# Loading the adjacency matrix through two hardware queues, one per half of the partitions, in 1 KB packets

## The chip, the cores and the metric

The kernel runs on one core of a Trainium2 chip. The metric is device microseconds of one execution. The core has TensorE (PE), VectorE (DVE), ScalarE (ACT), GpSimd (POOL) and SyncE (SP), each with its own instruction stream, and 16 DMA engines that all queues share. SP and ACT can each issue transfers to a hardware queue of their own; POOL has a software queue.

## The reference

Two graph layers in sequence over N = 4096 nodes with D = 128 features, both with the same dense 4096 x 4096 float32 matrix `adj`:

```
h = relu(layernorm(x))
x = x + L0(h, adj, weight, bias)      # hyperbolic layer; its heart is  adj @ x_tangent
h = relu(layernorm(x))
x = x + L1(h, context, adj, ...)      # attention layer
# L0: mx = h @ weight.T; per row tanh/artanh scalings; bias added in the ball; logmap -> x_tangent
#     support = adj @ x_tangent; per row scalings, relu
# L1: in_fts = context @ W_common.T; left = in_fts @ w_left + b_left; right likewise
#     logits = leaky(left[:, None] + right[None, :], 0.2); where adj <= 0: -inf; softmax; @ h; relu
```

`adj` is 64 MB. It is read from memory once: the first layer multiplies with its values, and its signs stay on the chip as an int8 mask for the second.

## The kernel before, in words

The rows of `adj` are taken in 8 chunks c of 512 rows, the columns in 32 blocks k of 128. There is a stage ahead of the chunks and there are two phases.

*Ahead of the chunks*, x (16 transfers, `load_nodes`, L301) and the context (16 transfers) are loaded by SP, and DVE, ACT, PE and POOL work out `xt`, the tangent vectors of all nodes; the last 28 of them are finished within chunk 0 (`bias_part` on ACT, L705, and `tangent` on DVE, L970).

*Phase 1* (`load` L321, `turn` L1047, `product` L611, `signs` L750). Per block of 512 rows by 128 columns: DVE turns it (`turn_block` L875, one 32x32-block transpose of 128x512 values, into a ring of TSLOTS = 4 turned blocks), PE multiplies `xt[:, k]` with it into a bank of PSUM (L619), and ACT writes the signs of two turned blocks into the mask (L758). A turned slot is free again when PE and ACT have read it. DVE's instruction order is fixed: beside the transposes of chunk c stand the steps that finish chunk c - 1 (`post_steps`, L979), each behind a block of a given number: relu behind 7, sums behind 12 and 13, `shrink` (L1001) behind 17, `residual` (L1016) behind 21 and 22, `variance` (L1034) behind 25, `affine` (L1040) behind 29. Two of them need POOL: `norms` (L514, between L996 and L1001) and `inverse_std` (L518, between L1034 and L1040). Between these POOL does the preparation of the second layer in pieces (`beside`, L503): eight pieces `left_or_right` (L452 and L457), then the sums and a store of `neg_left` to memory in 4-byte elements (L465), the largest value, and exponentials. ACT finishes a chunk with `normed` (L743), four instructions behind the last sign of the next chunk.

Loading: SP alone issues `adj`. A tile of the load ring is 16 rows by 128 columns for each partition (512-byte packets), 1 MB, four blocks k; the ring has XSLOTS = 4 tiles. A tile is four transfers of 256 KB, one for each group b of 32 partitions, and its place is asked for when DVE has turned all four blocks of the tile that was there (L328). Between tiles SP also issues the store (`store_x1`, L307) and the load (`load_x`, L313) of 512 rows of x.

*Phase 2* (`attend` L626, `edges` L779, `split` L1098) is the attention product over the mask; it loads only rows of x and of `neg_left`, and PE, DVE and ACT share it.

A node's number is made of (s, b, l, q): chunk s, group b of 32 partitions, l of 4, q within the group; this order is used for rows, columns, x, context and the output alike.

Of the kernel before, what the change touches and what calls it, by code (L numbers as in the profile page):

```python
# [44 lines left out]
Q = 32  # L45
NQ = P // Q
L = 4
CH = L * P
XSLOTS = 4
# [4 lines left out]
BESIDE = 8  # L54

# [21 lines left out]
def bass_two_graph_layers(nc, x, adj, weight, bias, context, w_common, w_left, b_left, w_right, b_right, out):  # L77
# [3 lines left out]
    NC = N // CH  # L81
    TH = NC * HALVES
# [3 lines left out]
    with ExitStack() as ctx:  # L86
# [10 lines left out]
        phase_1_bytes = XT_BYTES + XSLOTS * CH * L * 4 + TSLOTS * CH * 4  # L97
# [32 lines left out]
        loaded = view(room, o, [XSLOTS, L * NQ, L * Q], F32)  # L130
        o += XSLOTS * CH * L * 4
# [8 lines left out]
        assert nl_at == 4 * half_slot and (NC - XSLOTS) % XSLOTS == 0  # L140
# [97 lines left out]
        def nodes(t):  # L238
            return t.rearrange("(s b l q) d -> s b q l d", b=NQ, l=L, q=Q)

        x_n, out_n = nodes(x), nodes(out)
        x_l, cx_l = (t.rearrange("(s b l q) d -> l b q s d", b=NQ, l=L, q=Q) for t in (x, context))
        adj_n = adj.rearrange("(s r p) (g b j) -> s g b p r j", r=CH // Q, p=Q, b=NQ, j=L * Q)
# [56 lines left out]
        def _(sp):  # L300
            def load_nodes(t, src, into):  # L301
# [3 lines left out]
            load_nodes(x_in, x_l, x_in_sem)  # L305
# [15 lines left out]
            def load(c, _):  # L321


                rows = pick(adj_n, c)
                for g in range(NC):
                    if not (isinstance(c, int) and c == 0 and g < XSLOTS):

                        sp.wait_ge(block_turned, c * NK + L * (g - XSLOTS + 1))  # L328
                    for b in range(NQ):
                        sp.dma_start(loaded[b * Q:(b + 1) * Q, g % XSLOTS], rows[g, b]).then_inc(  # L330
                            adj_in[g % XSLOTS], 16)
                    if isinstance(c, int) and c == 0 and g == XSLOTS - 1:
                        load_nodes(cx, cx_l, cx_in)
# [14 lines left out]
            sp.wait_ge(block_turned, NC * NK - (XSLOTS - 1) * L)  # L348
# [220 lines left out]
        def _(pe):  # L569
# [85 lines left out]
        def _(act):  # L655
            act.dma_start(W_in, weight).then_inc(weights_in, 16)
            act.dma_start(b_colv, bias.rearrange("(d a) -> d a", a=1)).then_inc(weights_in, 16)
            act.dma_start(bias_b, bias.rearrange("(a d) -> a d", a=1).broadcast_to([P, D])).then_inc(weights_in, 16)

# [45 lines left out]
            def bias_part(k):  # L705

                if k >= XT_AHEAD:
                    act.wait_ge(xt_ready, k - XT_AHEAD + 1)
                nc.scalar.activation(fb[:, k % XT_AHEAD, :], hb, ACT.Copy, scale=sv[:, 14, k:k + 1]).then_inc(
                    fb_ready, 1)  # L710
# [39 lines left out]
            def signs(c, parity):  # L750
# [3 lines left out]
                mc = mask[:, c] if number else mask[:, bass.ds(c, 1)].rearrange("p o k i -> p (o k) i")  # L754
                for half in range(TH):
# [78 lines left out]
        def _(dve):  # L834
# [40 lines left out]
            def turn_block(c, k):  # L875
                g, l = k // L, k % L
                if l == 0:
                    dve.wait_ge(adj_in[g % XSLOTS], c * (16 * NQ * NC // XSLOTS) + 16 * NQ * (g // XSLOTS + 1))
# [91 lines left out]
            def tangent(k):  # L970

                dve.wait_ge(fb_ready, k + 1)
                v.scalar_tensor_tensor(out=xt[:, k, :], in0=mx[:, k, 0:D], scalar=T1[:, k:k + 1],  # L973
                                       in1=fb[:, k % XT_AHEAD, :], op0=ALU.mult, op1=ALU.add).then_inc(xt_ready, 1)
# [72 lines left out]
            def turn(c, parity):  # L1047
                number = isinstance(c, int)
                steps = {} if number and c == 0 else post_steps(c - 1)
                for k in range(NK):  # L1050
                    if not (number and c == 0 and k < TSLOTS):
                        turn_block(c, k)
                    if number and c == 0:
                        tangent(k)
# [144 lines left out]
```

## Time and profile before

| | us |
|---|---|
| median of 3 runs | 674.5 (673.03 to 675.14) |
| the profiled execution's own time | 676.54 |
| its span | 674.7 |

Mean granted clock of TensorE 0.941 of full speed. Busy shares of the span: PE 76%, DVE 81%, ACT 63%, POOL 34%. The page cuts the span into 40 slices of 16.9 us. DMA traffic is nearly all in slices 1 to 23, which are the stage ahead and phase 1; phase 2 follows, from about 386 us to the end. In windows of less than the span the same line has 40 slices of that window. "Idle before, releaser" tells what ended an engine's idle time; idle time of an engine that is not the bottleneck costs nothing.

### The profile page before, as it was taken

What the parts mean: (1) busy time and instruction counts of PE and PEld (TensorE: products, weight loads), DVE (VectorE), ACT (ScalarE), POOL (GpSimd) and SP (SyncE); (2) the same over time, 40 slices, a digit from 0 to 9 for tenths busy, and PEclk for the clock granted to TensorE, in tenths of its full rate; (3) what the DMA queues carried; (4) which work ended last, traced back from release to release, by engine and by line L of the source; (5) the groups of instructions that cost most, each with busy time, mean ns of one, the idle gap of its engine ahead of it and who ended that gap; (6) DMA issues with size and microseconds to landing.
All of it is one profiled execution on the core that took longest, in us unless ns stands there. A gap on an engine that the chain in (4) does not pass through costs nothing. (4 is left out here: it accounts for less than half of the span.)

```text
span 674.7 us, 9733 instructions
## 1 busy us (share of the span) xinstructions
PE 512.0 (76%) x2695; PEld 312.2 (46%) x2695; DVE 545.3 (81%) x1057; ACT 422.5 (63%) x553; POOL 226.9 (34%) x217
## 2 busy tenths in 40 slices
PE   1705986597589478687786855669998989899995
PEld 1602432242233223222232244458877878787875
DVE  4897957989697366574665799999999999999995
ACT  2946954273356245445354487849898888879881
POOL 5810067949948168000000075720101020202010
PEclk9966999799799699999999968888999999999998
DMA  9995999999999999999999701010101001011010
GB/s 180 214 223 111 213 214 213 222 213 213 181 217 152 169 216 225 213 213 223 214 219 215 141 17 32 1 32 17 32 17 33 18 30 47 16 31 31 0 31 16
DMA packets 164235, 84.51 MB, mean 125 GB/s; under 512 B 7248, under 2 KB 163152, under 8 KB 164208
## 3 DMA queue, kind: packets, MB, share of 16 engines
q1 hardware_dynamic: 163520, 83.91, 69.4%
q0 software_dynamic: 256, 0.15, 0.1%
q8 instruction: 11, 0.18, 0.1%
q10 hardware_dynamic: 432, 0.13, 0.1%
q14 instruction: 16, 0.13, 0.1%
HBM read 79.96 MB, written 4.21 MB: 125 GB/s over the span
## 5 line engine op out<-in xcount | busy, mean ns | idle before, releaser
L619 PE MATMUL ps<-room 128*128 128x512 f32 x512 | 254.0, 633 | 94.9 <-DVE room L884 72.5
L884 DVE STREAM_TRANSPOSE room<-room 128x512 f32<-128x512 f32 x256 | 169.6, 692 | 91.2 <-DMA room<-in_adj_dram 78.1
L758 ACT ACTIVATE mask<-room 128x1024 f32 (+1 forms) x128 | 135.0, 1055 | 160.0 <-DVE room L884 158.0
L619 PEld LDWEIGHTS ps<-room 128*128 128x128 f32 x512 | 93.8, 198 | 249.6 <-DVE room L884 168.6
L645 PE MATMUL ps<-room 128*128 128x258 f16 x1152 | 139.3, 282 | 29.6 <-DVE room L1126 29.6
L645 PEld LDWEIGHTS ps<-room 128*128 128x128 bf16 x1152 | 114.0, 100 | 53.6 <-DVE room L1126 35.2
L645 PE MATMUL ps<-room,mask 128*128 128x258 f16 x896 | 102.5, 275 | 9.4 <-DVE h_room L1140 6.3
L645 PEld LDWEIGHTS ps<-room,mask 128*128 128x128 bf16 x896 | 87.0, 98 | 23.6 <-DVE h_room L1140 8.0
L797 ACT ACTIVATE room<-mask 128x2048 bf16 (+1 forms) x36 | 68.5, 1902 | 13.9 <-PE ps L645 13.9
L554 POOL TENSOR_TENSOR h_room<-h_room 128x512 f32<-128x512 f32 x7 | 9.9, 1408 | 146.4 <-DVE post L1151 146.4
L797 ACT ACTIVATE mask<-mask 128x2048 bf16 (+1 forms) x28 | 53.3, 1903 | 5.0 <-PE ps L645 5.0
L452 POOL TENSOR_TENSOR mask<-mask 128x2048 f32<-128x2048 f32 x8 | 36.1, 4512 | 50.7 <-DVE room L973 50.5
L1116 DVE TENSOR_TENSOR room<-room 128x2048 bf16<-128x2048 bf16 x36 | 48.4, 1344 | 1.3 <-ACT room L797 0.4
L457 POOL TENSOR_TENSOR mask<-mask 128x1024 f32<-128x1024 f32 (+3 forms) x64 | 46.5, 726 | 5.0
L514 POOL TENSOR_TENSOR post<-post,powers 128x8 f32<-128x8 f32 x8 | 13.4, 1670 | 98.0 <-DVE post L996 98.0
L1116 DVE TENSOR_TENSOR mask<-mask 128x2048 bf16<-128x2048 bf16 x28 | 34.7, 1238 | 1.1
L827 ACT ACTIVATE h_room<-ps,factors 128x258 f32<-128x258 f32 x32 | 14.0, 471 | 33.0 <-PE ps L645 21.3
L1070 DVE TENSOR_SCALAR room<-room,r_col 128x512 bf16<-128x512 f32 x42 | 27.1, 686 | 0.0
L1125 DVE TENSOR_SCALAR room<-room 128x2048 bf16<-128x2048 bf16 x36 | 25.5, 708 | 0.2
L1126 DVE TENSOR_SCALAR room<-room 128x2048 bf16<-128x2048 bf16 x36 | 25.4, 704 | 0.0
L806 ACT ACTIVATE room<-room,r_col 128x512 bf16<-128x512 f32 x38 | 25.1, 709 | 0.0
L518 POOL TENSOR_TENSOR post<-post,powers 128x4 f32<-128x4 f32 x8 | 8.3, 1036 | 43.8 <-DVE post L1034 43.6
(164 smaller groups left out, 552.9 us busy)
## 6 DMA issues: line engine op xcount, KB each, us to landing
room<-in_adj_dram SPq DMA_DIRECT2D x256, 256.0 KB, 6.8
mask<-in_L_gnn_context_dram SPq DMA_DIRECT2D x16, 256.0 KB, 10.6
mask<-in_x_dram SPq DMA_DIRECT2D x16, 128.0 KB, 5.7
xk<-in_x_dram SPq DMA_DIRECT2D x32, 64.0 KB, 4.4
out_dram<-xk SPq DMA_DIRECT2D x32, 64.0 KB, 4.2
h_room<-out_dram SPq DMA_DIRECT2D x32, 64.0 KB, 2.5
out_dram<-h_room SPq DMA_DIRECT2D x28, 64.0 KB, 1.8
room<-neg_left SPq DMA_DIRECT2D x4, 256.0 KB, 3.6
```

Of the source, the lines that this page charges most:

```text
L452: side(nc.gpsimd.tensor_tensor(products, cx[:, ks, :], v_rows[:, w, :].unsqueeze(1).broadcast_to([P, BESIDE, C]), ALU.mult))
L457: side(nc.gpsimd.tensor_tensor(dst, products[:, :, 0:n], products[:, :, n:2 * n], ALU.add))
L619: pe.matmul(acc[parity], xt[:, k, :], turned[:, k % TSLOTS, :], start=(k == 0), stop=(k == NK - 1)).then_inc(block_multiplied, 1)
L645: mm = pe.matmul(ps[:, 2 * t + w, 0:GW], part[slot(c, g)][:, kk, t * P:(t + 1) * P], G[w][:, k, :], start=(k == 0), stop=(k == NK - 1))
L758: nc.scalar.activation(mc[:, half * HB:(half + 1) * HB, :], turned[:, slots:slots + HB, :], ACT.Sign).then_inc(half_signed, 1)
L797: nc.scalar.activation(neg[slot(c, g)], mc[:, g * L:(g + 1) * L, :], ACT.Relu, scale=4.0).then_inc(edges_ready, 1)
L806: ins = nc.scalar.activation(pos[slot(c, g)][:, kk, :], nl[parity], ACT.Sign, scale=-1.0, bias=r_col[:, k:k + 1])
L884: v.transpose(turned[:, k % TSLOTS, :].rearrange("p (l b i) -> p b l i", l=L, b=NQ), loaded[:, g % XSLOTS, :, l * Q:(l + 1) * Q].rearrange ...
L1070: ins = v.tensor_scalar(pos[slot(c, g)][:, kk, :], nl[parity], r_col[:, k:k + 1], -1.0, ALU.is_le, ALU.add)
L1116: v.tensor_tensor(pos_g, pos_g, neg_g, ALU.add).then_inc(coded, 1)
L1125: v.tensor_scalar(neg_g, pos_g, 3.0, None, ALU.is_equal)
L1126: v.tensor_scalar(pos_g, pos_g, 4.0, None, ALU.is_ge).then_inc(parts_ready, 1)
```

## The change

SP issues the transfers of partitions 0 to 63 (`LOW`), ACT those of partitions 64 to 127 (`HIGH`), for x and for `adj`; the context stays with SP. A tile of `adj` becomes 16 rows by 256 columns for each partition (1 KB packets), 2 MB, eight blocks, and the ring has two tiles (the same room). Transfers of `adj` are 512 KB; there are 128 of them, where there were 256. ACT issues a tile's high half behind the last sign of the tile that it replaces (in the last tile of a chunk also behind `normed`), and its loop over the chunks is written out. SP's store and load of x rows move from tiles 1 and 3 of 8 to tiles 0 and 1 of 4.

Node numbers are now made of (b, l, s, q). So a partition's 16 rows of a tile are 256 rows (4 MB of memory) apart, where they were 32 rows (512 KB), and the four groups b read columns 1024 apart. The columns of block k are those of xt and mask place `node(k)`; the mask is written with a stride.

```
-XSLOTS = 4
+XSLOTS = 2
+XB = 8
+LOW, HIGH = range(NQ // 2), range(NQ // 2, NQ)
+    NT = NK // XB
...
-        loaded = view(room, o, [XSLOTS, L * NQ, L * Q], F32)
+        loaded = view(room, o, [XSLOTS, L * NQ, XB * Q], F32)
...
-        adj_n = adj.rearrange("(s r p) (g b j) -> s g b p r j", r=CH // Q, p=Q, b=NQ, j=L * Q)
+        x_l, cx_l = (t.rearrange("(b l s q) d -> l b q s d", b=NQ, l=L, q=Q) for t in (x, context))
+        adj_n = adj.rearrange("(r s p) (b g j) -> s g b p r j", s=NC, p=Q, b=NQ, j=XB * Q)
+        def node(n):
+            return n % XB * L + n // XB
...
-                for g in range(NC):
+                for g in range(NT):
                     if not (isinstance(c, int) and c == 0 and g < XSLOTS):
-                        sp.wait_ge(block_turned, c * NK + L * (g - XSLOTS + 1))
-                    for b in range(NQ):
-                        sp.dma_start(loaded[b * Q:(b + 1) * Q, g % XSLOTS], rows[g, b]).then_inc(
-                            adj_in[g % XSLOTS], 16)
+                        sp.wait_ge(block_turned, c * NK + XB * (g - XSLOTS + 1))
+                    for b in LOW:
+                        sp.dma_start(loaded[b * Q:(b + 1) * Q, g % XSLOTS], rows[g, b]).then_inc(adj_in[g % XSLOTS], 16)
...
-                    if g == 1 and not (isinstance(c, int) and c < 2):
+                    if g == 0 and not (isinstance(c, int) and c < 2):
                         store_x1(c - 2)
-                    if g == 3 and not (isinstance(c, int) and c < 1):
+                    if g == 1 and not (isinstance(c, int) and c < 1):
                         load_x(c - 1)
...
-                    pe.matmul(acc[parity], xt[:, k, :], turned[:, k % TSLOTS, :],
+                    pe.matmul(acc[parity], xt[:, node(k), :], turned[:, k % TSLOTS, :],
...
+            def load_high(rows, g):
+                for b in HIGH:
+                    act.dma_start(loaded[b * Q:(b + 1) * Q, g % XSLOTS], rows[g, b]).then_inc(adj_in[g % XSLOTS], 16)
+            for l in range(L):
+                for b in HIGH:
+                    act.dma_start(by_l(x_in, l)[b * Q:(b + 1) * Q], x_l[l, b]).then_inc(x_in_sem[l], 16)
+            for g in range(XSLOTS):
+                load_high(adj_n[0], g)
...
                 for half in range(TH):
                     act.wait_ge(block_turned, c * NK + HB * (half + 1))
                     slots = half % HALVES * HB
-                    nc.scalar.activation(mc[:, half * HB:(half + 1) * HB, :], turned[:, slots:slots + HB, :],
+                    first = node(half * HB)
+                    nc.scalar.activation(mc[:, first:first + L + 1:L, :], turned[:, slots:slots + HB, :],
                                          ACT.Sign).then_inc(half_signed, 1)
...
                     if half in steps:
                         steps[half]()
+                    if (half + 1) % (XB // HB) == 0:
+                        tile = half // (XB // HB) + XSLOTS
+                        if tile < NT:
+                            load_high(rows, tile)
+                        elif further is not None:
+                            load_high(further, tile - NT)
-            chunked(act, signs)
+            for c in range(NC):
+                signs(c, c % 2)
...
             def turn_block(c, k):
-                g, l = k // L, k % L
+                g, l = k // XB, k % XB
```

## Rows read from the trace of the kernel before

**Rows 1.** The page: DMA busy tenths and GB/s in 40 slices.
```profile
DMA  9995999999999999999999701010101001011010
GB/s 180 214 223 111 213 214 213 222 213 213 181 217 152 169 216 225 213 213 223 214 219 215 141 17 32 1 32 17 32 17 33 18 30 47 16 31 31 0 31 16
```

**Rows 2.** Waits of all engines: waiter, awaited, us in total, times, longest.
```profile
DVE room L884 <- DMA room<-in_adj_dram: 78.1, 37, 10.7
```

**Rows 3.** Groups by line: shapes, count, busy us, mean ns, idle before, releasers.
```profile
L884 DVE STREAM_TRANSPOSE room<-room 128x512 f32<-128x512 f32 x256 | 169.6, 692 | 91.2 <-DMA room<-in_adj_dram 78.1 <-PE ps L619 8.6 <-ACT mask L758 2.4
L758 ACT ACTIVATE mask<-room 128x1024 f32 (+1 forms) x128 | 135.0, 1055 | 160.0 <-DVE room L884 158.0
```

**Rows 4.** Windows of 10 us: busy per engine, clock, DMA share, GB/s.
```profile
40.00:50.00 10.00, 0.00 (x0) 0.00 (x0) 8.48 (x37) 5.58 (x10) 0.00 (x0) 0.50 1.13 224
70.00:80.00 10.00, 10.00 (x25) 4.38 (x24) 10.00 (x24) 9.64 (x18) 0.00 (x0) 1.00 1.22 213
320.00:330.00 10.00, 6.80 (x15) 2.44 (x15) 6.78 (x13) 3.59 (x6) 1.64 (x1) 1.00 1.23 213
```

**Rows 5.** DMA view of 241 to 245 us, 0.1 us a slice.
```profile
GB/s 220 215 195 210 210 200 205 210 200 200 225 241 266 230 220 220 205 215 215 210 179 205 205 195 215 215 210 205 195 200 205 220 205 210 205 230 251 271 225 195
```

**Rows 6.** DMA view of 1.5 to 9.5 us, 0.2 us a slice.
```profile
GB/s 0 77 115 164 325 341 287 226 157 141 90 100 102 74 143 120 187 223 228 300 272 295 272 270 203 187 144 168 223 185 132 178 159 146 173 244 228 205 236 213
```

**Rows 7.** Timeline of 300 to 345 us: start, us, engine, line, what, idle before.
```profile
309.94 2.49 DVE L884 STREAM_TRANSPOSE room<-room 128x512 f32<-128x512 f32 x4 [2.28 <-DMA room<-in_adj_dram]
310.71 3.70 PE L619 MATMUL ps<-room 128*128 128x512 f32 x8 [0.63 <-DVE room L884]
...
318.31 0.19 PEld L619 LDWEIGHTS ps<-room 128*128 128x128 f32 x1 [0.24 <-issue]
...
318.74 0.19 PEld L619 LDWEIGHTS ps<-room 128*128 128x128 f32 x1 [0.24 <-issue]
```

**Rows 8.** Source view of the adj transfers: issue durations ns, then issue to landing.
```profile
L330 SPq DMA_DIRECT2D room<-in_adj_dram x256: 311/980/8402, 9.9 to 375.5; - x128
...
DMA to landing us min/median/max: 3.2/6.8/15.9
```

**Rows 9.** Timeline of 0 to 24 us: a DMA issued by ACT.
```profile
1.68 0.46 ACTq L658 DMA_DIRECT2D mask<-in_L_gnn_bias_dram  x1
```

**Rows 10.** Groups by line of ACT, 230 to 385 us.
```profile
L743 ACT ACTIVATE h_room<-xk,post 128x128 f32 x12 | 4.9, 478 | 0.0
```

**Rows 11.** Timeline of POOL, 75 to 240 us.
```profile
104.98 1.65 POOL L514 TENSOR_TENSOR post<-post,powers 128x8 f32<-128x8 f32 x1 [8.02 <-DVE post L996]
...
117.62 4.50 POOL L452 TENSOR_TENSOR mask<-mask 128x2048 f32<-128x2048 f32 x1
...
128.62 1.02 POOL L518 TENSOR_TENSOR post<-post,powers 128x4 f32<-128x4 f32 x1
...
149.54 1.65 POOL L514 TENSOR_TENSOR post<-post,powers 128x8 f32<-128x8 f32 x1 [9.00 <-DVE post L996]
...
194.01 1.65 POOL L514 TENSOR_TENSOR post<-post,powers 128x8 f32<-128x8 f32 x1 [8.88 <-DVE post L996]
```

**Rows 12.** Timeline of DVE, 134 to 300 us.
```profile
129.67 4.46 DVE L1040 SCALAR_TENSOR_TENSOR post<-mv,post 128x4 f32<-128x4 f32 x1 [0.70 <-POOL post L518]
...
211.92 0.12 DVE L1040 SCALAR_TENSOR_TENSOR post<-mv,post 128x4 f32<-128x4 f32 x1
...
227.50 2.49 DVE L884 STREAM_TRANSPOSE room<-room 128x512 f32<-128x512 f32 x4 [10.68 <-DMA room<-in_adj_dram]
```

**Rows 13.** Timeline of POOL, 230 to 340 us.
```profile
240.88 1.69 POOL L514 TENSOR_TENSOR post<-post,powers 128x8 f32<-128x8 f32 x1 [10.06 <-DVE post L996]
...
281.80 1.64 POOL L514 TENSOR_TENSOR post<-post,powers 128x8 f32<-128x8 f32 x1 [13.26 <-DVE post L996]
```

**Rows 14.** DMA view of 205 to 232 us: issues, KB, median us to landing.
```profile
neg_left<-mask POOLq DMA_DIRECT2D x1, 16.0 KB, 18.3
```

**Rows 15.** The chain of waits: start, us, piece.
```profile
384.40 1.23 DVE room L884 x2
```

More of the change, by code:

```diff
@@ L96, in bass_two_graph_layers @@
         XT_BYTES = NK * D * 4
-        phase_1_bytes = XT_BYTES + XSLOTS * CH * L * 4 + TSLOTS * CH * 4
+        phase_1_bytes = XT_BYTES + XSLOTS * CH * XB * 4 + TSLOTS * CH * 4
         phase_2_bytes = 2 * NK * GW * 2 + 3 * 2 * L * CH * 2
@@ L129, in bass_two_graph_layers @@
         o += NK * D * 4
[L130 to L131 removed]
+        loaded = view(room, o, [XSLOTS, L * NQ, XB * Q], F32)
+        o += XSLOTS * CH * XB * 4
         turned = view(room, o, [TSLOTS, CH], F32)
@@ L139, in bass_two_graph_layers @@
         nl_at = XT_BYTES
-        assert nl_at == 4 * half_slot and (NC - XSLOTS) % XSLOTS == 0
+        assert nl_at == 4 * half_slot and NT % XSLOTS == 0
         nl_even = view(room, nl_at, [CH], F32)
@@ L238, in nodes @@
         def nodes(t):
-            return t.rearrange("(s b l q) d -> s b q l d", b=NQ, l=L, q=Q)
+            return t.rearrange("(b l s q) d -> s b q l d", b=NQ, l=L, q=Q)
         x_n, out_n = nodes(x), nodes(out)
-        x_l, cx_l = (t.rearrange("(s b l q) d -> l b q s d", b=NQ, l=L, q=Q) for t in (x, context))
-        adj_n = adj.rearrange("(s r p) (g b j) -> s g b p r j", r=CH // Q, p=Q, b=NQ, j=L * Q)
+        x_l, cx_l = (t.rearrange("(b l s q) d -> l b q s d", b=NQ, l=L, q=Q) for t in (x, context))
+        adj_n = adj.rearrange("(r s p) (b g j) -> s g b p r j", s=NC, p=Q, b=NQ, j=XB * Q)
+        def node(n):
+            return n % XB * L + n // XB
         def pick(view_, c):
@@ L300, in _, with load_nodes @@
         def _(sp):
-            def load_nodes(t, src, into):
+            def load_nodes(t, src, into, blocks):
                 for l in range(L):
-                    for b in range(NQ):
+                    for b in blocks:
                         sp.dma_start(by_l(t, l)[b * Q:(b + 1) * Q], src[l, b]).then_inc(into[l], 16)
-            load_nodes(x_in, x_l, x_in_sem)
+            load_nodes(x_in, x_l, x_in_sem, LOW)
             def store_x1(p):
@@ L324, in load @@
                 rows = pick(adj_n, c)
-                for g in range(NC):
+                for g in range(NT):
                     if not (isinstance(c, int) and c == 0 and g < XSLOTS):
-                        sp.wait_ge(block_turned, c * NK + L * (g - XSLOTS + 1))
-                    for b in range(NQ):
-                        sp.dma_start(loaded[b * Q:(b + 1) * Q, g % XSLOTS], rows[g, b]).then_inc(
-                            adj_in[g % XSLOTS], 16)
+                        sp.wait_ge(block_turned, c * NK + XB * (g - XSLOTS + 1))
+                    for b in LOW:
+                        sp.dma_start(loaded[b * Q:(b + 1) * Q, g % XSLOTS], rows[g, b]).then_inc(adj_in[g % XSLOTS], 16)
                     if isinstance(c, int) and c == 0 and g == XSLOTS - 1:
-                        load_nodes(cx, cx_l, cx_in)
-                    if g == 1 and not (isinstance(c, int) and c < 2):
+                        load_nodes(cx, cx_l, cx_in, range(NQ))
+                    if g == 0 and not (isinstance(c, int) and c < 2):
                         store_x1(c - 2)
-                    if g == 3 and not (isinstance(c, int) and c < 1):
+                    if g == 1 and not (isinstance(c, int) and c < 1):
                         load_x(c - 1)
@@ L346, in _ @@
             sp.wait_ge(nl_stored, 16)
-            sp.wait_ge(block_turned, NC * NK - (XSLOTS - 1) * L)
+            sp.wait_ge(block_turned, NC * NK - (XSLOTS - 1) * XB)
             neg_left_row(0, 0)
@@ L708, in bias_part @@
                     act.wait_ge(xt_ready, k - XT_AHEAD + 1)
-                nc.scalar.activation(fb[:, k % XT_AHEAD, :], hb, ACT.Copy, scale=sv[:, 14, k:k + 1]).then_inc(
+                at = node(k)
+                nc.scalar.activation(fb[:, k % XT_AHEAD, :], hb, ACT.Copy, scale=sv[:, 14, at:at + 1]).then_inc(
                     fb_ready, 1)
@@ L754, in signs @@
                 mc = mask[:, c] if number else mask[:, bass.ds(c, 1)].rearrange("p o k i -> p (o k) i")
+                rows = pick(adj_n, c)
+                further = None if number and c == NC - 1 else adj_n[c + 1] if number else pick(adj_n, c + 1)
                 for half in range(TH):
@@ L969, in _, with tangent @@
             dve.wait_ge(tangent_scales, 1)
-            def tangent(k):
-                dve.wait_ge(fb_ready, k + 1)
+            def tangent(n, k):
+                dve.wait_ge(fb_ready, n + 1)
                 v.scalar_tensor_tensor(out=xt[:, k, :], in0=mx[:, k, 0:D], scalar=T1[:, k:k + 1],
-                                       in1=fb[:, k % XT_AHEAD, :], op0=ALU.mult, op1=ALU.add).then_inc(xt_ready, 1)
+                                       in1=fb[:, n % XT_AHEAD, :], op0=ALU.mult, op1=ALU.add).then_inc(xt_ready, 1)
             POST = 6
@@ L1053, in turn @@
                     if number and c == 0:
-                        tangent(k)
+                        tangent(k, node(k))
                     if k in steps:
```

2 lines of the change are left out of this document (1 added, 1 removed).

## The prediction, made before the changed kernel was run

> **What bounds the kernel now.** I read the page's slices first. The DMA digits are at 9 or near it from slice 1 to slice 23 and almost nothing after; in the full slices the core moves 213 to 216 GB/s, and it moves no more in any slice than 225 [rows 1]. So the change can act on the first 386 us only, and there the question is who waits for the loads. By the waits, DVE stands 78.1 us for `adj`, in 37 waits, the longest 10.7 us [rows 2]; nothing else holds its transposes for long (8.6 and 2.4 us), and ACT in turn waits 158.0 us for DVE [rows 3]. 78.1 us is the ceiling of the gain, unless something else speeds up as well.
>
> Is 213 GB/s a limit of the packet, of memory, or of where the data lands? Three readings. The context is loaded in 1 KB packets to 32 partitions at a time and goes at 224 GB/s, `adj` in 512-byte packets at 213 [rows 4]: twice the packet gives 5%. Seen in slices of 0.1 us, the `adj` stream has two humps in 4 us, 241-266-230 and 251-271-225, 2.5 us apart [rows 5]. A transfer of 256 KB takes 1.23 us at 213 GB/s, so a hump stands at every second change of transfer, not at each: that fits changes between the lower and the upper 64 partitions, where for some 0.3 us both are being written, and not those within a half. And early, where the loads of x share the DMA engines with 128-partition loads of ACT and POOL, slices reach 287 to 341 and 270 to 300 GB/s with packets mostly of 512 bytes [rows 6]. I take it that one half of the partitions takes in some 213 to 224 GB/s, and that both together take more.
>
> The Trainium skill speaks on both sides here. "SBUF — State Buffer", section "Door 1", gives 8 of 16 ports and about 218 GB/s to partitions 0 to 63; the trace agrees with 213 to 224. The same page, section "Can I just issue two DMAs to hit both halves?", says no: two at a time gained 6%, and "DMA: Bandwidth & Descriptors", section "Rules for kernel authors", says of two transfers to disjoint halves not to bother. The humps speak against that for this stream, and it is the first rival below.
>
> **The change part by part.**
>
> *The rate R with both halves open.* Bounds from the nearest rows: 213 (nothing gained) and 341 (the highest slice). The humps' 266 and 271 are the same loads, but averaged over a moment that is partly one-sided, and with the smaller packet. I take R = 290, with 250 and 340 as the forecast's own ends.
>
> *The ring of two tiles.* A tile (2.1 MB) is asked for when the eight blocks in its place are turned, and has to be there when the other tile has been turned. If L is the time from that release to the landing and T the time DVE needs for a landed tile, two tiles take L + T, unless DVE, PE or the DMA engines need more. T: four transposes take 2.49 us [rows 7], eight 5.0; in 320 to 330 us DVE is busy 6.78 us [rows 4] with 8.1 blocks (5.0 us of transposes), so 1.7 us of other steps per tile: T = 6.7. L: the shortest landing of 256 KB is 3.2 us [rows 8], less 1.2 of data at 213: 2.0 fixed. Data: 2.1 MB at 290, 7.2 us. ACT issues the high half behind its sign (1.055 us, [rows 3]) and one issue of 0.46 [rows 9]; meanwhile the low half is alone at about 213, which costs 1.5 x (1 - 213/290) = 0.4. In the last tile of a chunk `normed`, 4 x 0.48 us [rows 10], stands ahead too: a quarter of about 1.4, 0.35. L = 10.0. So a tile takes (10.0 + 6.7)/2 = 8.35 us, 1.044 per block. The other limits are lower: PE's records start 0.43 us apart, two to a block, 0.86 per block [rows 7]; the data alone is 7.2 us per tile. With R = 340, L = 9.0 and a block takes 0.98; with 250, L = 11.2 and a block 1.12.
>
> *ACT's issues.* Two per tile, 0.92 us at the 0.46 of its own row. Behind them stand the next signs, which DVE needs four blocks later. Per tile in the late chunks ACT then has 4.2 of signs, about 1 of other steps and 0.9 of issues in 8.35 us: hidden. At most two tiles' high halves, four transfers, are ever outstanding, and SP had 6.8 / 1.23 = 5.5 in flight before an issue was held (its median issue of 980 ns is that hold, its minimum 311) [rows 8]; so I cost no hold. If that cover is gone, an issue costs ACT what it cost SP, about 1 us, 8.4 at worst.
>
> *Stage ahead.* x arrives over both halves; its first group has to wait for ACT's three small loads (0.46 each). I cost -0.5 to +1, zero. ACT's first compute instruction waits for DVE's statistics of x, which need x landed, and so stands well behind its issues.
>
> *Chunk 0.* ACT is saturated (9.64 of 10 us busy, [rows 4]) with signs and `bias_part`. Four times 0.92 us of issues go on top: +3.7. The two-tile ring adds about 1 at its third tile, mostly beside it. Behind chunk 0 DVE used to wait some 8 us for loads before block 13 of chunk 1; there I get it back, and `norms` starts about 105, as before (104.98, [rows 11]).
>
> *Chunks 1 to 3: POOL's.* This is where the expected gain stays away. From `norms` at 104.98 POOL runs two pieces of 10.9 (one starts with the 4.50 at 117.62) and ends `inverse_std` at 129.64: 24.7 us [rows 11]. Then `affine` on DVE stands 4.46 us [rows 12], as long as POOL's next L452. These 29.1 us cover blocks 14 to 29, which need 14 to 18 us of loads' or DVE's time: faster loads change nothing. The other 16 blocks take 15.4 us (to 149.54), already PE's pace, 0.86 to 0.96 a block, from tiles that were loaded during the stand. With the two-tile ring only blocks up to 7 of the next chunk are there; block 31 is turned 1.2 us behind the stand's end, its place lands 10.0 + 1.1 later, and block 8 wants it at +9.4: +2 us for each such half chunk. The period was 44.5 (149.54 to 194.01); I take 46.5, twice: 198.
>
> *The end of that stretch.* Blocks 14 to 29 of chunk 3 took 17.9 us (194.01 to 211.92), bound by DVE and its stands: 18, so 216. Then 29.0 us to the next `norms` at 240.88 [rows 13]: here the store of `neg_left` in 4-byte elements is in flight for 18.3 us [rows 14], and DVE waits 10.68 us for `adj` [rows 12]. Undisturbed this stretch costs 15.4 + 2. Two queues with twice the packet put more `adj` bytes between two turns of the store; nothing in the trace prices it. Between 17.4 and 29 I take 22: 238.
>
> *Chunks 4 to 7.* From `norms` at 240.88 to the last transpose's end at 385.63 [rows 15] are 144.8 us for 115 blocks (1.26 each; a chunk 40.9, by 281.80 - 240.88). At 1.044: 120.1, so 358.
>
> *The rest.* Phase 2 has no part in the change: the strided mask write, `node(k)` and the written-out ACT loop add no instruction per block; 0, at most ±1.
>
> **The sum.** Phase 1 ends at 358 in place of 385.6: -27.6. The profiled execution took 676.54 for a span of 674.7, 2.0 above the median of the runs shown; 676.5 - 27.6 = 648.9, and on the median's scale 674.5 - 27.6 = 647. By terms: chunk 0 and the start 0, chunks 1 and 2 +4, the `neg_left` stretch -7, chunks 4 to 7 -24.7. Best ends together (R = 340, no ring loss, 17.4 in the `neg_left` stretch) give 632; worst (R = 250, 29 there, +3 at chunk 0) 669.
>
> **Rivals.**
>
> *The halves don't add.* If each engine works its two queues off in turn and every packet waits for its port, R stays at the context's 224 [rows 4]. Then the data of a tile is 9.4 us, L = 12.2, and a tile takes 9.45: 1.19 per block, 136.5 us for the 115; the early half chunks lose 4.5 instead of 2, the `neg_left` stretch 27: 385, that is 674, up to 681 if the engines idle in part of L. For it: the pages above, and that the engines are shared. Against it: [rows 5, 6].
>
> *Memory at a stride of 4 MB (the slower side).* A partition's 16 rows of a tile are now 4 MB apart, 512 KB before. If rows so far apart meet in the same part of memory, R falls for every `adj` transfer. From about R = 224 down this decides: 63 MB are to come, so each 10% off costs 28 us, and 200 GB/s gives about 708. Against it: neighbouring partitions, which the 16 engines read side by side, stay 16 KB apart; no row shows a stride above 512 KB. The Trainium skill, "DMA: Bandwidth & Descriptors", section "Latency and other measured facts", has half the rate for a pitch of 4 MiB against 512 KiB, but between the partitions of a transfer; no row here shows it, and by its half R would be near 110 and the time above 900.
>
> *ACT is held by its issues.* If two transfers of 512 descriptors cost ACT more than about 2.5 us per tile, it paces DVE and comes late with the high half; 28 tiles with 1 us too much are 28 us, and the time lands between 650 and 690. For it: SP's 980 ns and 8.4 us. Against it: only four transfers outstanding.
>
> *More than forecast.* R near 340 and the `neg_left` stall gone: below 634.
>
> **Chances.** Forecast 0.56 (own range 634 to 669, all of it faster); better 0.06; halves don't add 0.17 (faster 0.03, no change 0.05, slower 0.09); stride 0.09, slower; ACT held 0.12 (0.06, 0.01, 0.05). A measurement of this kernel tells about 0.3% (2 us) from no change. Faster 0.71, no change 0.06, slower 0.23. The range runs from 632, with 0.05 below, to 682, which holds most of the first rival and leaves out the stride and half of ACT's bad end, some 0.13.
>
> **What would show it.** Right: two hardware queues with about equal bytes and slices of 280 to 300 GB/s in chunks 4 to 7, with gaps between tiles; `norms` 46 us apart in chunks 1 to 3 and some 33 apart in 4 to 7; DVE's waits for `adj` of 1.5 to 3 us, once per eight blocks. Wrong: slices that stay at 213 to 224 (first rival) or fall below (second); ACT's DMA issues of 1 us and more (third); `norms` less than 44 us apart in chunks 1 to 3, which would mean that POOL did not bound them; or a phase 2 of another length than 289 us.

## The result: 880 us, slower by 31%, and the profile after

The changed kernel takes 880.24 us (median of 4 runs, 875.07 to 881.91), the kernel before in the same session 673.76 (671.54 to 675.14). The ratio is 1.306, interval 1.299 to 1.312. The forecast of 647 was wrong in its sign; the time lies far outside the range of 632 to 682. Ratios here and below compare runs near each kernel's fastest; a single run that took clearly longer than its others is given with its time.

The page of the profiled execution (875.07 us, span 873.3): DMA busy tenths and GB/s in 40 slices, now of 21.8 us each, and the DMA queues with packets, MB and share of the 16 engines.

```profile
DMA  7914786577777887778767877720000101001000
GB/s 200 246 48 53 145 145 136 123 124 133 129 132 155 120 59 165 107 136 159 154 117 143 168 110 161 134 73 1 25 25 18 33 26 37 12 24 36 24 23 13
...
q1 hardware_dynamic: 59968, 49.30, 29.0%
q10 hardware_dynamic: 36400, 34.74, 21.9%
```

The same bytes go over two queues, as meant. But where [rows 1] has 213 to 216 GB/s, there are now 107 to 168 in the full slices (59 in slice 15, where the store of `neg_left` is in flight), and the DMA digit stands mostly at 7 or 8, not 9. Phase 1's loads run to slice 27 of 21.8 us, where they ran to slice 23 of 16.9 us.

The view of waits, all engines, then SP's queue (waiter, awaited, us, times, longest):

```profile
DVE room L912 <- DMA room<-in_adj_dram: 260.9, 30, 19.2
...
SPq L326 <- DMA out_dram<-xk: 66.9, 6, 15.3
```

DVE's wait for `adj` has grown from 78.1 us in 37 waits [rows 2] to 260.9 in 30, by 183 us. The span has grown by 198.6. SP's wait at L326 is for a store of x rows that shares the slow stream; behind it stands SP's half of the next tile. Of DVE's 260.9 us, 217.9 are put down to SP's halves and 43.0 to ACT's. Experiment 1 will show that the loss comes without this wait too. The rest is shown by POOL's `norms` (L520, L514 before), one per chunk:

```profile
147.43 1.65 POOL L520 TENSOR_TENSOR post<-post,powers 128x8 f32<-128x8 f32 x1 [17.38 <-DVE post L1024]
213.90 1.65 POOL L520 TENSOR_TENSOR post<-post,powers 128x8 f32<-128x8 f32 x1 [28.39 <-DVE post L1024]
283.16 1.65 POOL L520 TENSOR_TENSOR post<-post,powers 128x8 f32<-128x8 f32 x1 [23.78 <-DVE post L1024]
357.57 1.69 POOL L520 TENSOR_TENSOR post<-post,powers 128x8 f32<-128x8 f32 x1 [11.64 <-DVE post L1024]
424.11 1.64 POOL L520 TENSOR_TENSOR post<-post,powers 128x8 f32<-128x8 f32 x1 [21.18 <-DVE post L1024]
488.25 1.64 POOL L520 TENSOR_TENSOR post<-post,powers 128x8 f32<-128x8 f32 x1 [37.28 <-DVE post L1024]
...
549.04 1.64 POOL L520 TENSOR_TENSOR post<-post,powers 128x8 f32<-128x8 f32 x1 [35.11 <-DVE post L1024]
```

A chunk takes 61 to 74 us where it took 41 to 47 [rows 11, 13], in POOL's chunks as in the later ones. The last transposes of phase 1 start at 582.31 and take 1.48 us, so it ends at 583.8 in place of 385.6: 198.2 of the 198.6 us. Phase 2 takes 289.5 us, as before. So the loss lies in phase 1, in the loads: that is the second rival's picture (memory at a stride of 4 MB), which had a chance of 0.09. What follows had to show whether it was the stride, or one of the other things that the change did to the loads.

### The profile page after: what moved, and what is told of

Read it like the earlier page. It is cut to its first block, busy times and chain, and to the rows that moved or that the text cites. A ratio compares the mean times of both kernels' runs of the same rounds, so it can differ in the third digit from the quotient of the medians.

```text
span 873.3 us, 9067 instructions
## 1 busy us (share of the span) xinstructions
PE 550.2 (63%) x2695; PEld 335.0 (38%) x2695; DVE 532.8 (61%) x1057; ACT 422.8 (48%) x553; POOL 227.0 (26%) x217
## 4 chain that ended last, share of the span: by engine, by line
DMA 41%; DVE 31%; PE 12%; issue 7%; SPq 4%; ACTq 2%; ACT 2%; POOL 1%; DVEq 1%; POOLq 0%
DMA room<-in_adj_dram 38%; PE ps L625 9%; DVE room L1098 4%; DVE room L1144 4%; DVE mask L1098 3%; DVE room L912 3%; DVE room L1154 3%; DVE mask L1144 3%; DMA out_dram<-xk 3%; PE ps L651 2%; SPq L318 2%; DVE mask L1154 2%; ACTq L669 1%; SPq L337 1%; DVE h_room L1168 1%
## 5 line engine op out<-in xcount | busy, mean ns | idle before, releaser
L625 PE MATMUL ps<-room 128*128 128x512 f32 x512 | 289.2, 723 | 247.6 <-DVE room L912 209.6
L912 DVE STREAM_TRANSPOSE room<-room 128x512 f32<-128x512 f32 x256 | 171.6, 696 | 298.0 <-DMA room<-in_adj_dram 260.9
L779 ACT ACTIVATE mask<-room 128x1024 int8<-128x1024 f32 x128 | 135.0, 1055 | 354.2 <-DVE room L912 353.4
L625 PEld LDWEIGHTS ps<-room 128*128 128x128 f32 x512 | 113.7, 231 | 414.7 <-DVE room L912 290.4
L651 PE MATMUL ps<-room 128*128 128x258 f16 x1152 | 141.9, 285 | 28.4 <-DVE room L1154 28.4
L520 POOL TENSOR_TENSOR post<-post,powers 128x8 f32<-128x8 f32 x8 | 13.4, 1669 | 174.8 <-DVE post L1024 174.8
## 6 DMA issues: line engine op xcount, KB each, us to landing
room<-in_adj_dram ACTq DMA_DIRECT2D x64, 512.0 KB, 17.4
```

The source lines that it names most:

```text
L625: pe.matmul(acc[parity], xt[:, node(k), :], turned[:, k % TSLOTS, :], start=(k == 0), stop=(k == NK - 1)).then_inc(block_multiplied, 1)
L651: mm = pe.matmul(ps[:, 2 * t + w, 0:GW], part[slot(c, g)][:, kk, t * P:(t + 1) * P], G[w][:, k, :], start=(k == 0), stop=(k == NK - 1))
L779: nc.scalar.activation(mc[:, first:first + L + 1:L, :], turned[:, slots:slots + HB, :], ACT.Sign).then_inc(half_signed, 1)
L912: v.transpose(turned[:, k % TSLOTS, :].rearrange("p (l b i) -> p b l i", l=L, b=NQ), loaded[:, g % XSLOTS, :, l * Q:(l + 1) * Q].rearrange ...
```

## The experiments

Four things changed in the loads: the distance of a partition's rows, the packet with the groups' columns apart, the tile and ring, the two queues. Theory A: the distance alone. Theory B: two queues or the small ring. Theory C: the columns.

**1. The distance alone, on the kernel before.**

```
-adj_n = adj.rearrange("(s r p) (g b j) -> s g b p r j", r=CH // Q, ...)
+adj_n = adj.rearrange("(r s p) (g b j) -> s g b p r j", s=NC, ...)
```

> The kernel before (one queue, 512-byte packets, four tiles), with one thing changed: the 16 rows of adj that a partition takes in a tile are 256 rows (4 MB) apart instead of 32 (512 KB). The product is then with wrongly ordered rows. Theory A (memory serves rows 4 MB apart slowly, and that alone made the changed kernel slow): adj falls from 213 GB/s to what the changed kernel shows, 120 to 160, and the time goes to 800 to 900 us. Theory B (two rings on the same 16 DMA engines get in each other's way, or the two-tile ring exposes each landing): nothing changes, 674 us within 5. Theory C (the four groups reading columns 4 KB apart): 674 us too.

Measured: 888.35 us (884.83 to 891.42), ratio 1.317, interval 1.310 to 1.324. One queue, small packets and the old ring, and yet the whole loss. Its waits, and two windows of 20 us (busy per engine, clock, DMA share, GB/s):

```profile
DVE room L884 <- DMA room<-in_adj_dram: 323.3, 57, 15.1
...
320.00:340.00 20.00, 11.85 (x22) 5.27 (x23) 7.20 (x13) 6.87 (x10) 0.65 (x2) 0.67 0.60 128
...
400.00:420.00 20.00, 11.47 (x23) 4.52 (x23) 6.03 (x10) 6.11 (x9) 0.00 (x0) 0.76 0.65 128
```

128 GB/s in place of 213, with the engines' share at 0.60 to 0.65 instead of 1.22 [rows 4]. The packets themselves are not recorded as longer. SP's queue in the kernel before, then in this one (packets, MB, share of 16 engines' span):

```profile
q1 hardware_dynamic: 163520, 83.91, 69.4%
```

```profile
q1 hardware_dynamic: 163520, 83.91, 48.1%
```

That is 45.8 ns a packet (0.694 x 16 x 674.7 us by 163520) against 41.9. The time lost stands between the recorded packets, so a DMA share that falls need not mean that the engines had too little to do.

**2. The changed kernel without the distance.**

```
-adj_n = adj.rearrange("(r s p) (b g j) -> s g b p r j", s=NC, ...)
+adj_n = adj.rearrange("(s r p) (b g j) -> s g b p r j", s=NC, ...)
```

> The changed kernel (two queues, 1 KB packets, two tiles of 2 MB), with one thing undone: a partition's 16 rows are 512 KB apart again; the groups' columns stay 1024 apart. Rows and columns are then in different orders, so the product is of wrongly ordered rows. Theory A: the two halves add, slices of 280 to 300 GB/s in chunks 4 to 7, and the sum of the prediction holds, plus some 9 us for ACT's held issues at the start: 640 to 670 us. Theory B: 850 to 880 us as the changed kernel. Theory C: 850 to 880 as well.

Measured: 662.28 us (659.10 to 667.56), ratio 0.983, interval 0.975 to 0.991. With one access pattern undone, 218 us are gone; theories B and C fall. The DMA view of 340 to 360 us, 0.5 us a slice:

```profile
GB/s 238 240 344 352 346 336 219 330 365 264 240 350 346 340 225 234 338 352 352 340 352 312 213 230 221 242 262 336 352 350 270 225 242 354 346 344 354 180 29 106
```

Here the forecast's mechanism can be read off: plateaus of mostly 336 to 354, with both queues carrying equal bytes (0.10 MB each in 341.2 to 341.8 us), and valleys of 213 to 242. Split by queue, the valleys are of two kinds. In some one queue carries nearly all: ACT's 0.08 MB against 0.02 from 340.0 to 340.4, SP's alone 0.11 MB from 343.0 to 343.5 and from 351.0 to 351.5, there in packets of some 512 bytes, those of x rows. In others both carry the same (0.04 MB each from 340.4 to 340.8, 0.06 from 345.0 to 345.5) and the rate is 218 to 240 all the same; that isn't explained. The mean of the window is 287 GB/s; I had taken 290.

**3. The change's first part alone: two queues.**

```
-                    for b in range(NQ):
+                    for b in LOW:
                         sp.dma_start(loaded[...], rows[g, b])
...
+                    if half % HALVES == HALVES - 1:      # ACT, behind the sign of a tile's last blocks
+                        ...load_high(...)
```

> The kernel before with SP issuing adj for partitions 0 to 63 and ACT for 64 to 127, behind its sign of a tile's last two blocks; 512-byte packets, four tiles of 1 MB, rows and columns in the old order, x by SP alone. Theory A: the halves add; R about 265 (the humps), chunks 4 to 7 about 33 us each instead of 41, time 640 to 660. Theory B: slower than 700. Theory C: 640 to 660.

Measured: 648.77 us (647.38 to 653.92), ratio 0.966, interval 0.959 to 0.972. The order of nodes, the packets and the ring are the old ones. The later `norms` are 30.5 to 31.6 us apart, where 33 was expected. It is also 13.5 us faster than experiment 2, so the longer packet in a ring of two tiles brought nothing that shows.

**4. 1 MB on the kernel before.**

```
-adj_n = adj.rearrange("(s r p) (g b j) -> s g b p r j", ...)
+adj_n = adj.rearrange("(t r h p) (g b j) -> t h g b p r j", h=2, ...)   # chunk c: t = c // 2, h = c % 2
```

> The kernel before with a partition's 16 rows 64 rows (1 MB) apart instead of 512 KB, SP's loop over the chunks written out for it; the product is of wrongly ordered rows. Theory A with a cost that grows with the stride: between 680 and 780 us; theory A with a cost that begins above 1 MB: 674 within 5. Theories B and C: 674 within 5.

Measured: 675.03 us (10 runs, 672.58 to 677.41), ratio 1.001, interval 0.999 to 1.004. One queue moves some 213 GB/s here and so would hide a loss that begins above that.

**5. The same distance, not a power of two.** Two accounts of "4 MB" were left: it is far, or it is an exact power of two.

```
-adj.rearrange("(r s p) ...")                       # r: 256 rows
+adj[0:16 * 255].rearrange("(r x) ...", x=255)[...]  # r: 255 rows, 4 MB less 16 KB
```

> The changed kernel with one thing changed: a partition's 16 rows are 255 rows apart, 4 MB less 16 KB, instead of 256 (each chunk reads 32 rows of 16 such stripes; the product is of wrongly ordered rows). The bytes, the packets, the queues, the tiles and the distance are as in the changed kernel. Theory A1 (rows an exact multiple of a large power of two apart meet in the same part of memory): as with 512 KB, 655 to 670 us, and packets of 1 KB take some 46 to 60 ns in the middle and under 100 at the ninth decile. Theory A2 (it is the distance: anything some MB apart is slow, whatever the exact number): 850 to 890 us.

Measured: 792.74 us (790.81 to 796.30), ratio 1.179, interval 1.173 to 1.185. Neither account: 88 us better than 256 rows, 130 worse than 32.

**6. Half the distance, on the changed kernel.**

```
-adj_n = adj.rearrange("(r s p) (b g j) -> s g b p r j", s=NC, ...)
+adj_n = adj.rearrange("(t r h p) (b g j) -> t h g b p r j", h=4, ...)   # chunk c: t = c // 4, h = c % 4
```

> The changed kernel with a partition's 16 rows 128 rows (2 MB) apart instead of 256 (wrongly ordered rows). Theory A1, if each doubling of the stride halves the number of places that a tile's rows fall on: between 690 and 800 us. If the cost begins only at 4 MB: 655 to 670. A2 says between 700 and 850.

Measured: 760.76 us (five runs at 754.54 to 764.51; the profiled one took 904.57 at a granted clock of 0.564, and its profile isn't read), ratio 1.130, interval 1.125 to 1.135.

**7. A whole kernel with 1 KB packets and 1 MB.** Nodes numbered (t, b, l, h, q), chunk c = 2t + h: the 256 columns of a packet stay adjacent, and the 16 rows are 64 apart.

```
-"(b l s q) d -> s b q l d"      adj "(r s p) (b g j) -> s g b p r j"
+"(t b l h q) d -> t h b q l d"  adj "(t r h p) (g b j) -> t h g b p r j"
```

> A whole kernel with the change's two queues, 1 KB packets and two tiles of 2 MB, but nodes numbered so that a partition's 16 rows are 64 rows (1 MB) apart and the four groups' columns of a tile lie side by side; x and the context are loaded in twice as many transfers for it. If 1 MB costs nothing at the rate of two queues either: 655 to 668 us, as with 512 KB. If 1 MB costs some of the rate above 213 GB/s, which one queue could not show: 670 to 720.

Measured: 669.92 us (10 runs, 667.23 to 676.47), ratio 0.996, interval 0.992 to 1.000. It is 8 us above experiment 2; that the stride costs these isn't separated from the 32 transfers more at the start.

From here a rule could be formed. A matrix row is 16 KB. The 32 rows that the partitions of a group take cover the lowest five bits of the row number. 32, 64, 128 and 256 rows between a partition's own rows let bits 5 to 7 take 8, 4, 2 and 1 values within a chunk; 255 rows, where row = 256r + (p - r) from the chunk's first row on, two, with about three quarters of the rows in one of them. The times were 662, 670, 761, 880 and 793. The bits are a description that fits these times, not a known address map. A rule with bit 8 added (16, 8, 4, 2 and 4 values) ranks the five no differently, and the part of bit 5 rests on the 8 us just named.

**8. The rule tested: 3.5 MB.**

```
-stripes of 255 rows
+stripes of 224 rows (7 x 32: all eight values of bits 5 to 7)
```

> The changed kernel with a partition's 16 rows 224 rows (3.5 MB) apart (chunk c reads the first 32 rows of 16 such stripes from row 32 c on, some rows twice over the kernel; wrongly ordered). What the runs suggest so far: a matrix row is 16 KB, and memory is spread by bits of the row number above the lowest five; 32, 64, 128, 256 rows apart leave 8, 4, 2, 1 different values of bits 5 to 7 in one chunk's rows, 255 leaves 2, and the times were 662, 670, 761, 880, 793. 224 = 7 x 32 leaves all 8. By that theory 655 to 670 us. By the theory that distance costs (more than 2 MB apart is slow): 790 to 900.

Measured: 659.69 us (659.37 to 668.25), ratio 0.981, interval 0.975 to 0.987. Nearly as far as 4 MB, and as fast as 512 KB. Distance is not it. (With bit 8 added, 224 rows have all values too.) The page's slices:

```profile
GB/s 195 285 168 0 140 193 265 204 122 272 221 121 269 171 90 241 238 284 286 275 272 275 96 1 31 1 33 17 33 17 33 40 20 35 16 31 31 0 31 16
```

**9. The start.** In experiments 2 and 3 ACT began late. The timeline of ACT in experiment 3:

```profile
2.17 13.41 ACTq L663 DMA_DIRECT2D room<-in_adj_dram  x8
15.62 1.28 ACT L684 ACT_TABLE_LOAD   x1 [15.62 <-issue]
18.07 1.65 ACT L684 ACTIVATE mask<-mask 128x128 f32<-128x128 f32 x4 [1.18 <-DVE mask L856]
```

Eight transfers took ACT 13.41 us, 1.68 each: a hold like SP's [rows 8], now in front of ACT's first work. The edit: SP issues the first four tiles whole.

> The version with two queues, 512-byte packets and four tiles, with the first four tiles issued whole by SP, so that ACT issues no adj ahead of its first compute instruction. If ACT's held issues at the start (its first compute instruction came at 15.6 and 18.1 us there instead of 12.8) cost what they delay, 2 to 3 us come back: 645 to 647. If they were hidden, or if the first tiles come later through one queue, nothing: 648.8 within 2.

Measured: 638.92 us (three runs at 635.59 to 639.13, one at 658.30), ratio 0.947, interval 0.941 to 0.953. It gave 10 us, not 2 to 3. The first `norms` of experiment 3 and of this version:

```profile
107.08 1.65 POOL L515 TENSOR_TENSOR post<-post,powers 128x8 f32<-128x8 f32 x1 [3.28 <-DVE post L1011]
```

```profile
98.49 1.65 POOL L515 TENSOR_TENSOR post<-post,powers 128x8 f32<-128x8 f32 x1 [3.09 <-DVE post L1008]
```

8.6 of the 10 are there: ACT's first compute instruction comes 5 us earlier (at 13.10), and chunk 0 starts sooner. The edit took away two things at once, though. In experiment 3 x itself landed later, since ACT's `adj` transfers moved beside it. DVE's first instruction on x, of experiment 3 and of this version:

```profile
10.46 1.65 DVE L864 BATCH_NORM_STATS2 mask<-mask 128x6 f32<-128x128 f32 x8 [10.46 <-DMA mask<-in_x_dram]
```

```profile
8.20 1.64 DVE L861 BATCH_NORM_STATS2 mask<-mask 128x6 f32<-128x128 f32 x8 [8.20 <-DMA mask<-in_x_dram]
```

So some 2.3 of the 5 us are x's landing and some 2.7 ACT's hold. This is the version to take; it beats both kernels.

**10. The store in 4-byte elements.**

```
-pool.dma_start(nl_dram.rearrange("k p -> p k"), neg_l, ...)
+pool.dma_start(nl_dram, ident[0:NK, :])
```

> The version with two queues, 512-byte packets and the first tiles by SP, with the store of neg_left (16 KB in 4096 elements of 4 bytes) replaced by one of the same size in 32 rows of 512 bytes from another tile, at the same place of POOL's order; the second layer then works with wrong numbers. DVE waited 9.9 us for adj in one piece in that stretch. If the small elements alone hold the DMA engines: the stretch between the third and the fourth norms falls from 48 to 33 to 38 us and the time from 639 to 625 to 630. If the stretch is long for another reason (POOL's reduction of the maximum): 639 within 3.

Measured: 631.44 us (630.68 to 634.54), ratio 0.937, interval 0.934 to 0.940. The third and the fourth `norms`, of experiment 9 and of this one:

```profile
188.48 1.65 POOL L515 TENSOR_TENSOR post<-post,powers 128x8 f32<-128x8 f32 x1 [9.18 <-DVE post L1008]
...
229.29 0.38 POOL L475 PARTITION_ALL_REDUCE mask<-mask  x1 [12.55 <-issue]
237.03 1.68 POOL L515 TENSOR_TENSOR post<-post,powers 128x8 f32<-128x8 f32 x1 [7.37 <-issue]
```

```profile
187.90 1.65 POOL L515 TENSOR_TENSOR post<-post,powers 128x8 f32<-128x8 f32 x1 [9.07 <-DVE post L1008]
...
222.10 0.38 POOL L475 PARTITION_ALL_REDUCE mask<-mask  x1 [6.11 <-issue]
229.89 1.68 POOL L515 TENSOR_TENSOR post<-post,powers 128x8 f32<-128x8 f32 x1 [7.41 <-issue]
```

48.6 us become 42.0, not 33 to 38: the store costs 6.6 us. Behind it stands the other thing I had named. The fourth `norms` follows an idle time of 7.4 us that ends in "issue", so POOL itself came late from its reduction, not DVE. The store's 6.6 us come by the same way: POOL's idle time ahead of the reduction is 12.55 us with the small elements and 6.11 without.

The DMA engines suffer as well, and here ACT was held a second time. The stretch in experiment 9, ACT and then DVE:

```profile
210.95 5.81 ACTq L663 DMA_DIRECT2D room<-in_adj_dram  x1
...
216.79 5.10 ACTq L663 DMA_DIRECT2D room<-in_adj_dram  x1
221.93 1.06 ACT L763 ACTIVATE mask<-room 128x1024 int8<-128x1024 f32 x1 [9.21 <-issue]
```

```profile
224.07 2.49 DVE L896 STREAM_TRANSPOSE room<-room 128x512 f32<-128x512 f32 x4 [8.72 <-ACT mask L763]
```

Two issues of ACT took 5.81 and 5.10 us, its next sign stood 9.21 us behind them, and DVE stood 8.72 us for the sign. With the store in rows no issue there takes more than 0.51 us, and from 200 to 232 us the core moves 260 GB/s in place of 174. In experiment 9 this hold stays under POOL's reduction: DVE's sums are there at 231.2 us, POOL comes at 237.0.

**11. Halves or queues?**

```
-LOW, HIGH = range(NQ // 2), range(NQ // 2, NQ)
+LOW, HIGH = (0, 2), (1, 3)
```

> The same version with the groups dealt out otherwise: SP issues the partitions 0 to 31 and 64 to 95, ACT 32 to 63 and 96 to 127, so each queue has work in both halves and the two queues begin in the same half. If the gain comes from both halves being written at a time: the queues run side by side within one half, and the time goes back towards 674, to 655 to 675. If two queues gain by themselves, whatever their partitions: 639 within 4.

Measured: 661.11 us (658.36 to 665.61), ratio 0.981, interval 0.976 to 0.985. Against experiment 9 this gives back 22 us, though two queues issue the same transfers. Windows of 20 us, of experiment 9 (10 us each) and of this one:

```profile
310.00:320.00 10.00, 9.81 (x22) 3.85 (x22) 9.14 (x24) 7.72 (x11) 1.01 (x1) 1.00 1.20 276
320.00:330.00 10.00, 10.00 (x27) 4.48 (x26) 7.08 (x12) 6.57 (x9) 0.00 (x0) 1.00 1.20 281
```

```profile
300.00:320.00 20.00, 17.42 (x42) 6.76 (x40) 12.35 (x20) 11.99 (x16) 1.64 (x1) 1.00 1.21 253
```

253 GB/s is more than 213. That the queues drift apart and both halves are then open in part is my reading; no run shows it.

**12. One queue, halves in turn.**

```
-for b in range(NQ):
+for b in (0, 2, 1, 3):
```

> The kernel before with SP alone issuing a tile's four transfers in the order of groups 0, 2, 1, 3 instead of 0, 1, 2, 3, so that every transfer changes the half. If both halves can only be open at a change of transfer, for 0.3 us each as in the humps: there are twice as many changes, R goes from 213 to 220 to 235, time 655 to 668. If one queue keeps both halves open as well as two do (the engines get out of step): 640 to 650. If order means nothing: 674 within 3.

Measured: three runs at 664.92 to 666.82 and one at 648.70, against 674.49 before, all four at the same granted clock (0.944 to 0.945). The three are inside what I expected of twice as many changes, the fourth inside what I expected if one queue keeps both halves open as well as two do. So order means something, but which of the two accounts holds isn't settled. The profile is of a run of 664.92 us. Its DMA view of 241 to 245 us, 0.1 us a slice, to be laid beside [rows 5]:

```profile
GB/s 230 246 225 215 220 215 246 236 236 236 236 236 251 220 241 225 230 230 225 220 230 241 210 241 230 241 230 205 225 241 230 230 225 246 225 251 230 220 225 215
```

The valleys between the humps, down to 179, are gone; all slices are at 205 to 251, with a mean of 230. So order alone in one queue is worth some 8 to 10 us in three runs and 26 in the fourth, against 25 for the two queues on halves in experiment 3 and 35 in experiment 9.

## Why the prediction was wrong, step by step

**The step that failed is R.** "The rate R with both halves open" was bounded below at 213, "nothing gained", by rows of loads whose rows lay 512 KB apart at most. The change moved them to 4 MB, and I kept this out of the term and made it a rival at 0.09. R was 107 to 168. From 75 us, where the first tile behind the two of the start is issued, to 576 us, where the last has landed, the core moves 134 GB/s on the mean; the 30 tiles take 501 us, 16.7 each and 2.09 per block, where the forecast had 7.2 us of data in 8.35 us a tile and 1.044 per block. The measured rate accounts for the result: phase 1 ends at 583.8 and not at 358.

The first rival has a slip beside it: at R = 224 its L adds up to 11.8, not 12.2, since the low half's lead costs 0.1 there and not 0.4. That moves its 674 by some -4 us and decides nothing.

The reason that I gave against the rival was wrong as a reason. "Neighbouring partitions stay 16 KB apart" is true, and it covers only five bits of the row number; experiments 5, 6 and 8 show that bits above them matter. And I let "no row shows a stride above 512 KB" count against the rival, when it was only silence. A rate that only untested addresses would have should have widened the range downward, as I did for other costs without a row.

The Trainium skill had spoken: "DMA: Bandwidth & Descriptors", section "Latency and other measured facts", gives 207 GB/s at a row pitch of 512 KiB, 164 at 2 MiB and 103 at 4 MiB, measured between the partitions of copies. I set it aside because here the stride is within a partition. In this kernel too 4 MB gives 128 GB/s where 512 KB gives 213 (experiment 1), a factor of 0.60 against the 0.50 of the Trainium skill; by that half I had worked out over 900 us, and 880 came. The Trainium skill's remedy in the same place, a pitch off by 4 KiB, can't be tried within a partition, since a row of `adj` is 16 KB; the nearest to it, 16 KB less, brought 88 of 218 us back, and 512 KB less all of it. As to the rule of the Trainium skill, "DMA: Bandwidth & Descriptors", section "Rules for kernel authors", that two transfers to disjoint halves are not worth it, the measurement decides the other way for this stream: plateaus of 336 to 354 GB/s with both queues at work against 213 to 242, and 25 us of 674 in experiment 3, 35 in experiment 9.

**The other steps** can be checked on experiment 2, which differs from the changed kernel in the distance alone. POOL's `norms` there, one a chunk:

```profile
112.21 1.65 POOL L520 TENSOR_TENSOR post<-post,powers 128x8 f32<-128x8 f32 x1 [6.26 <-DVE post L1024]
...
158.36 1.65 POOL L520 TENSOR_TENSOR post<-post,powers 128x8 f32<-128x8 f32 x1 [10.52 <-DVE post L1024]
...
205.21 1.65 POOL L520 TENSOR_TENSOR post<-post,powers 128x8 f32<-128x8 f32 x1 [11.22 <-DVE post L1024]
...
258.66 1.69 POOL L520 TENSOR_TENSOR post<-post,powers 128x8 f32<-128x8 f32 x1 [9.00 <-DVE post L1024]
...
292.74 1.64 POOL L520 TENSOR_TENSOR post<-post,powers 128x8 f32<-128x8 f32 x1 [6.86 <-DVE post L1024]
...
325.17 1.64 POOL L520 TENSOR_TENSOR post<-post,powers 128x8 f32<-128x8 f32 x1 [17.91 <-DVE post L1024]
...
357.06 1.64 POOL L520 TENSOR_TENSOR post<-post,powers 128x8 f32<-128x8 f32 x1 [17.53 <-DVE post L1024]
```

- *Chunks 1 to 3, POOL's:* 46.2 and 46.9 us, predicted 46.5. Faster loads give nothing there. The two-tile ring costs its 2 us or near it: with four tiles (experiment 9) the same two periods are 45.2 and 44.8.
- *Chunks 4 to 7:* 34.1, 32.4 and 31.9, predicted 33.4. Right.
- *Start and chunk 0:* first `norms` at 112.21, predicted 105. Two terms at zero failed. ACT's issues ahead of its first work were costed at nothing, but its eight transfers of x took 7.27 us and the four of `adj` behind them 8.04, so its first work starts at 17.53. And x over both halves was costed at -0.5 to +1, but DVE's first instruction on it starts at 10.62 and not at 7.88, with `adj` loads beside it.
- *The stretch with the `neg_left` store:* 53.5 us, predicted 40. I expected two queues with larger packets to push past the store. They don't: DVE waits 19.09 us there in one piece. The floor of 17.4 us that I gave the second half of the stretch was wrong too: with the small elements gone the stretch is still 42.0 us (experiment 10), and POOL's reduction, which had no term in the sum, ends it.

```profile
243.54 2.49 DVE L912 STREAM_TRANSPOSE room<-room 128x512 f32<-128x512 f32 x4 [19.09 <-DMA room<-in_adj_dram]
```

These two misses, +7 and +13, are more than the distance from 647 to 662. The way from the fourth `norms` to the end of the last transpose (374.3) takes some back: 115.7 us, predicted 120.1. *ACT behind its sign*, a lag in my L, did not exist: its issues start with the sign, not behind it.

```profile
313.35 1.06 ACT L766 ACTIVATE mask<-room 128x1024 int8<-128x1024 f32 x1 [0.42 <-DVE room L899]
313.36 0.86 ACTq L663 DMA_DIRECT2D room<-in_adj_dram  x2
```

That row is from experiment 3. *Phase 2* kept its length, as predicted.

What stays open: which parts of memory the row bits select, since only times were measured; whether the 8 us between 1 MB and 512 KB are the stride's, and with them which bits count; why one queue with the halves in turn gave 649 us once and 665 three times; and why some short stretches of the changed kernel reach 246 GB/s and others 67 to 90 with the same pattern.

## What to carry to other kernels

When a change renumbers rows to get a longer packet, write down the address of what all engines read at the same time, before and after, and see which address bits still vary; here the longer packet brought nothing that shows and the bits that stood still cost 218 us. Loads to 32 partitions at a time moved 213 GB/s in one queue, so let two queues own one half each. Keep the issues of the first tiles out of the compute engine that is needed first, and look for its issues wherever the transfers are slowed: an engine that issues can be held by them. A bound taken from existing rows bounds only addresses like those in the rows.

## What the runs showed of the hardware that was not expected

- The rate of loads depends on the addresses read together, and not on their distance. The times go with the number of values that bits 5 to 7 of the 16 KB row number take: eight values 660 to 662 us (512 KB and 3.5 MB alike), four 670, two 761 and (unevenly) 793, one 880, all with two queues and 1 KB packets. Whether it is these three bits isn't shown.
- Loads slowed in this way show no longer packets (41.9 ns against 45.8 in experiment 1) but a smaller DMA share, 0.60 for 1.22.
- With a queue for each half of the partitions, both at work move 336 to 354 GB/s with packets of 1 KB; with one carrying nearly all the rate is 213 to 243.
- An issue can hold the engine that makes it: 1.68 us per transfer of 256 KB on ACT at the start, 5.81 and 5.10 us beside the store in 4-byte elements, 0.43 otherwise (0.86 for two). That a full queue is the reason is inferred.
- A store of 16 KB in 4-byte elements cost 6.6 us where one in rows of 512 bytes did not; the core moved 174 GB/s around it, 260 without.
- TensorE's granted clock averaged 0.833 of full speed in the changed kernel against 0.941: it was 0.58 from 360 to 380 us, where PE was busy for 5.28 of 20 us, and 0.92 from 500 to 520, where it was busy for 16.07, and the matmul of L625 took 723 ns in place of 633.
